# A two-pass product with a 5120 x 5120 matrix: h of a panel interleaved with t of the next, one landing ring, second reads on one queue

## The reference

```python
h = relu(layernorm(x))                                  # 5120 x 64
e = concat(par_u[0]*par_u[1] * (diag_u * h_u @ W_u) + h_u,     # first 2048 rows
           par_i[0]*par_i[1] * (diag_i * h_i @ W_i) + h_i)     # other 3072 rows
g = adj @ (adj.T @ e)                                   # two passes over adj
out = x + layernorm(g) * ln_gamma + ln_beta + h
```

## Time and profile before

| | |
|---|---|
| median of three runs | 540.03 us (538.85 to 540.18) |
| profiled execution | 538.86 us |
| its span | 537.0 us |
| busy: TensorE | 445.0 us, 83% |
| busy: VectorE | 343.5 us, 64% |
| busy: ScalarE | 312.5 us, 58% |
| moved | 139.43 MB, mean 260 GB/s |
| SyncE's queue (q1) | 123.28 MB, 63.1% of 16 engines' span |
| ScalarE's queue (q10) | 15.82 MB, 10.6% |

### The profile page before, as it was taken

One profiled execution on the slowest core, in us unless ns is written; L12 is line 12 of the kernel. 1 busy time (PEld: TensorE's weight loads), 2 busy tenths in 40 slices (PEclk: granted clock), 3 DMA queues, 4 the chain that ended last, 5 costly groups with the idle time before them and its releaser, 6 DMA issues.

```text
span 537.0 us, 5378 instructions
## 1 busy us (share of the span) xinstructions
PE 445.0 (83%) x2108; PEld 179.7 (33%) x2108; DVE 343.5 (64%) x338; ACT 312.5 (58%) x415; POOL 26.9 (5%) x30
## 2 busy tenths in 40 slices
PE   0747554599969989999969799997899898779996
PEld 0313222243423334324423333433343332334433
DVE  2635199473999941499991149999118999701742
ACT  2365830856699924069993207998324699622242
POOL 1011330000000000000000000000000000001132
PEclk9968795899979999999989899998999999799999
DMA  7966109685965979996957699795979968772911
GB/s 222 404 259 264 56 0 379 169 234 165 366 253 214 408 284 206 324 371 253 415 205 281 191 319 372 269 415 206 330 262 315 392 243 338 276 251 63 302 52 59
DMA packets 63112, 139.43 MB, mean 260 GB/s; under 512 B 4208, under 2 KB 37488, under 8 KB 63088
## 3 DMA queue, kind: packets, MB, share of 16 engines
q1 hardware_dynamic: 45360, 123.28, 63.1%
q10 hardware_dynamic: 17728, 15.82, 10.6%
HBM read 137.78 MB, written 1.31 MB: 259 GB/s over the span
## 4 chain that ended last, share of the span: by engine, by line
PE 29%; ACT 22%; DMA 22%; DVE 18%; issue 6%; ACTq 1%; SPq 1%; DVEq 0%
ACT ready L369 20%; DMA nat<-in_adj_dram 17%; PE tT_ps L673 11%; PE h_ps L731 10%; DVE ready L544 8%; DVE ready L533 7%; PE tr_ps L662 5%; DMA ready<-in_adj_dram 3%; DMA diag_sb<-in_L_gnn_diag_i_dram 2%; ACT ready L379 1%; PE tr_ps L710 1%; PE tT_ps L686 1%; ACTq L239 1%; SPq L239 1%; DVE tT_sb L550 1%
## 5 line engine op out<-in xcount | busy, mean ns | idle before, releaser
L369 ACT ACTIVATE ready<-nat 32x1024 f32<-32x1024 f32 x225 | 237.4, 1055 | 65.2 <-PE h_ps L731 47.0
L673 PE MATMUL tT_ps<-nat,e_sb 128*64 128x512 f32 x800 | 199.6, 646 | 31.8 <-DMA nat<-in_adj_dram 28.9
L544 DVE STREAM_TRANSPOSE ready<-ready 128x2048 f32<-128x2048 f32 x80 | 179.5, 2287 | 24.4 <-ACT ready L369 18.2
L731 PE MATMUL h_ps<-ready,t_quads 128*64 128x512 f32 x640 | 178.4, 604 | 7.9 <-DVE ready L544 7.9
L533 DVE COPY ready<-nat 32x1024 f32<-32x1024 f32 x175 | 121.1, 692 | 8.7 <-PE h_ps L731 6.0
L673 PEld LDWEIGHTS tT_ps<-nat,e_sb 128*64 128x64 f32 x800 | 62.1, 147 | 141.4 <-issue 101.8
L731 PEld LDWEIGHTS h_ps<-ready,t_quads 128*64 128x64 f32 x640 | 56.9, 139 | 94.5 <-issue 93.2
L379 ACT ACTIVATE ready<-tr_ps 128x512 f32<-128x512 f32 x80 | 44.0, 595 | 71.9 <-PE tr_ps L662 71.7
L731 PE MATMUL h_ps<-ready,t_blocks 128*64 128x512 f32 x160 | 70.0, 593 | 0.7 <-DVE t_blocks L554 0.7
L662 PE MATMUL tr_ps<-ident,nat 128*128 128x128 f32 x320 | 49.0, 302 | 15.2 <-ACT ready L379 15.2
L662 PEld LDWEIGHTS tr_ps<-ident,nat 128*128 128x128 f32 x320 | 38.6, 154 | 47.4 <-issue 27.9
(11 more groups left out here) (54 smaller groups left out, 118.8 us busy)
## 6 DMA issues: line engine op xcount, KB each, us to landing
nat<-in_adj_dram SPq DMA_DIRECT2D x50, 2048.0 KB, 9.6
ready<-in_adj_dram SPq DMA_DIRECT2D x30, 512.0 KB, 10.3
ready<-in_adj_dram ACTq DMA_DIRECT2D x30, 512.0 KB, 10.5
x_sb<-in_x_dram SPq DMA_DIRECT2D x5, 256.0 KB, 8.7
out_dram<-x_sb SPq DMA_DIRECT2D x10, 128.0 KB, 1.8
ready<-in_L_gnn_W_u_dram SPq DMA_DIRECT2D x2, 16.0 KB, 10.1
ready<-in_L_gnn_W_i_dram SPq DMA_DIRECT2D x2, 16.0 KB, 9.3
gamma_sb<-in_L_gnn_ln_gamma_dram ACTq DMA_DIRECT2D x1, 32.0 KB, 2.6
```

The lines of the kernel that those rows point to most:

```text
L369: last = nc.scalar.activation(dst, src, ACT.Copy)
L544: last = nc.vector.transpose(part, part)
L673: last = nc.tensor.matmul(tT_ps[half * D:(half + 1) * D, :], e_sb[:, g * RB + r, :], nat_slot(p, g)[:, r, half * BANK:(half + 1) * BANK], ...
L731: last = nc.tensor.matmul(h_ps[k][half * D:(half + 1) * D, :], t[:, b, :], tile, start=(p == 0 and b == 0), stop=True, skip_group_check=True)
```

## The change

The same work is cut and ordered in another way.

- `KIND`: groups 0, 5, 8 are read a second time, 1, 2, 3, 4, 6, 9 are moved (six, not five), 7 alone is turned by TensorE. `BANKS` pairs (2,4), (0,1), (3,6), (5,9), (7,8).
- ScalarE takes 8 to 10 of the 16 blocks of a move, by group (`ACT_MOVES`), 53 a panel.
- Buffers: `landing`, a ring of 5 slots for natural and second reads in the one order `LOADS`; `kept`, 7 slots, one for each group that is not read twice. In panel 0 two natural reads (5, 6) land in slots of `kept` (`EARLY`). A second read is turned in its landing slot and holds it until its bank of h is summed.
- All natural reads go out on SyncE's queue, all four transfers of each second read on ScalarE's.
- TensorE's order alternates banks of h of panel p with groups of t of panel p + 1. Both turns of t come before bank 0.
- `t_quads` and `t_blocks` are copied by ScalarE, not VectorE.
- In the head ScalarE's first move goes in pieces of three blocks, the weights and second unit of x are read ahead of the first group, and the moves of groups 6 and 9 of panel 0 come after t. In the tail all turns come ahead of the first `norm_h`.

```diff
-    KIND = ("read", "move", "read", "move", "read", "move", "turn", "move", "turn", "move")
+    KIND = ("read", "move", "move", "move", "move", "read", "move", "turn", "read", "move")
     MOVES = tuple(g for g in range(GROUPS) if KIND[g] == "move")
-    TURNS = tuple(g for g in range(GROUPS) if KIND[g] == "turn")
+    TURN = KIND.index("turn")
     READS = tuple(g for g in range(GROUPS) if KIND[g] == "read")
-    BANKS = ((1, 3), (5, 7), (6, 9), (0, 8), (2, 4))
-    H_ORDER = (1, 3, 5, 7, 9, 6, 8, 0, 2, 4)
-    FIRST_ORDER = tuple(range(GROUPS))
-    NATURAL = 4
-    TURNED = 8
-    ACT_MOVES = 9
+    KEPT = tuple(g for g in range(GROUPS) if KIND[g] != "read")
+    BANKS = ((2, 4), (0, 1), (3, 6), (5, 9), (7, 8))
+    LANDING = 5
+    ACT_MOVES = {1: 8, 2: 10, 3: 9, 4: 8, 6: 8, 9: 10}
     MOVE_BLOCKS = tuple((a, b) for b in range(NQ) for a in range(NQ))
     BATCH = 2
-    BATCHES = tuple((g, b) for g in TURNS for b in range(0, BLOCKS, BATCH))
-    BESIDE_FIRST = {(7, 0): 0, (7, 1): 1, (8, 0): 2, (8, 1): 3, (9, 0): 4, (9, 1): 5}
-    BESIDE = {(6, 0): 0, (6, 1): 1, (7, 0): 2, (7, 1): 3, (8, 0): 4, (8, 1): 5}
-    HELD = (6, 7)
+    EARLY = {5: 6, 6: 9}
+    LOADS = [(0, g, False) for g in range(GROUPS) if g not in EARLY]
+    for p in range(PANELS):
+        LOADS.append((p, READS[0], True))
+        if p < LAST:
+            LOADS += [(p + 1, 0, False), (p + 1, 1, False), (p + 1, 2, False)]
+        LOADS.append((p, READS[1], True))
+        if p < LAST:
+            LOADS.append((p + 1, 3, False))
+        LOADS.append((p, READS[2], True))
+        if p < LAST:
+            LOADS += [(p + 1, g, False) for g in range(4, GROUPS)]
...
-        nat = sb("nat", [P, NATURAL, SLOT])
-        ready = sb("ready", [P, TURNED, SLOT])
+        landing = sb("landing", [P, LANDING, SLOT])
+        kept = sb("kept", [P, len(KEPT), SLOT])
...
+        def landing_slot(p, g, second):
+            return landing[:, LOADS.index((p, g, second)) % LANDING, :]
+        def nat_rows(p, g):
+            slot = kept_slot(EARLY[g]) if p == 0 and g in EARLY else landing_slot(p, g, False)
+            return slot.rearrange("p (r c) -> p r c", r=RB)
+        def turned_rows(p, g):
+            return landing_slot(p, g, True) if KIND[g] == "read" else kept_slot(g)
...
+        def wait_landing_free(eng, p, g, second):
+            n = LOADS.index((p, g, second)) - LANDING
             if n >= 0:
-                p0, g0 = n // GROUPS, order(n // GROUPS)[n % GROUPS]
-                eng.wait_ge(t_summed, t_count(p0, g0))
-                if KIND[g0] == "move":
-                    eng.wait_ge(moved_act, move_count(p0, g0))
-                    eng.wait_ge(moved_dve, move_count(p0, g0))
-                if KIND[g0] == "turn":
-                    eng.wait_ge(tr_filled, tile_count(p0, g0) + BLOCKS)
-        def wait_ready_free(eng, p, g):
-            n = p * GROUPS + H_ORDER.index(g) - TURNED
-            if n >= 0:
-                eng.wait_ge(h_summed, h_count(n // GROUPS, H_ORDER[n % GROUPS]))
-        EGO = ready[:, TURNED - 1, :]
-        w_blk = ready[:, TURNED - 2, 0:2 * P].rearrange("p (s m) -> p s m", s=2)
-        FREE = nat[:, loads_before(LAST, READS[-2]) % NATURAL, :]
-        c_blk = nat[:, loads_before(LAST, READS[-1]) % NATURAL, 0:P]
-        cg_blk = nat[:, loads_before(LAST, READS[-1]) % NATURAL, P:2 * P]
+                p0, g0, second0 = LOADS[n]
+                if second0:
+                    eng.wait_ge(h_summed, h_count(p0, g0))
+                else:
+                    eng.wait_ge(t_summed, t_count(p0, g0))
+                    if KIND[g0] == "move":
+                        eng.wait_ge(moved_act, move_count(p0, g0))
+                        eng.wait_ge(moved_dve, move_count(p0, g0))
+                    if KIND[g0] == "turn":
+                        eng.wait_ge(tr_filled, tile_count(p0) + BLOCKS)
+        def wait_kept_free(eng, p, g):
+            if p:
+                eng.wait_ge(h_summed, h_count(p - 1, g))
+                return
+            if g in (TURN, KEPT[-1]):
+                eng.wait_ge(e_ready, PAIRS)
+            for g0, at in EARLY.items():
+                if at == g:
+                    eng.wait_ge(t_summed, t_count(0, g0))
+                    if KIND[g0] == "move":
+                        eng.wait_ge(moved_act, move_count(0, g0))
+                        eng.wait_ge(moved_dve, move_count(0, g0))
...
-            def second(p, g):
-                sp.wait_ge(t_summed, t_count(p, g))
-                if p == 0 and g == READS[0]:
-                    sp.wait_ge(e_ready, PAIRS)
-                wait_ready_free(sp, p, g)
-                load_second(sp, p, g, range(0, NQ // 2))
             load_x(0)
-            natural(0, 0)
+            load_x(1)
             sp.wait_ge(w_zeroed, 1)
             for s, W in enumerate((W_u, W_i)):
                 for half in range(2):
                     sp.dma_start(w_blk[half * D:(half + 1) * D, s, half * D:(half + 1) * D], W[:, :]).then_inc(w_in, 16)
-            for u in range(1, PAIRS):
+            natural(0, 0)
+            for u in range(2, PAIRS):
                 load_x(u)
-            for g in FIRST_ORDER[1:]:
+            for g in range(1, GROUPS):
                 natural(0, g)
-            for p in range(PANELS):
-                second(p, READS[0])
-                if p < LAST:
-                    natural(p + 1, H_ORDER[0])
-                second(p, READS[1])
-                second(p, READS[2])
-                if p < LAST:
-                    for g in H_ORDER[1:]:
-                        natural(p + 1, g)
+            for p in range(1, PANELS):
+                for g in range(GROUPS):
+                    natural(p, g)
...
             def second(p, g):
-                act.wait_ge(t_summed, t_count(p, g))
-                if p == 0 and g == READS[0]:
-                    act.wait_ge(e_ready, PAIRS)
-                wait_ready_free(act, p, g)
-                load_second(act, p, g, range(NQ // 2, NQ))
+                wait_landing_free(act, p, g, True)
+                load_second(act, p, g, range(NQ))
...
+            def take_quads(p):
+                act.wait_ge(t_turned, 2 * p + 1)
+                if p:
+                    act.wait_ge(h_summed, p * PAIRS)
+                nc.scalar.activation(t_quads[:, :, :], rows64(tT_ps[:, :]), ACT.Copy).then_inc(quads_ready, 1)
+            def take_blocks(p):
+                act.wait_ge(t_turned, 2 * p + 2)
+                if p:
+                    act.wait_ge(h_summed, h_count(p - 1, TURN))
+                nc.scalar.activation(t_blocks[:, :, :], rows64(tT_ps[:, :]), ACT.Copy).then_inc(blocks_ready, 1)
...
+                if u + 1 < PAIRS:
+                    squares(u + 1)
                 egoT_copy(u)
-                if u == 0:
-                    squares(1)
-                if u == 1:
-                    move(0, MOVES[0])
-                if u == 3:
-                    move(0, MOVES[1])
+                if 1 <= u < PAIRS - 1:
+                    move(0, 1, 3 * (u - 1), min(3 * u, ACT_MOVES[1]))
...
+            move(0, 2)
+            move(0, 3)
+            move(0, 4)
+            second(0, READS[0])
             turn_back(0, 0)
             turn_back(0, 1)
+            take_tT(0)
             turn_back(0, 2)
             for p in range(PANELS):
+                take_quads(p)
+                turn_back(p, 3)
+                take_blocks(p)
+                if p == 0:
+                    move(0, 6)
+                move(p, 9)
+                second(p, READS[1])
                 if p < LAST:
+                    move(p + 1, 1)
+                second(p, READS[2])
+                if p < LAST:
+                    move(p + 1, 2)
+                    move(p + 1, 3)
+                    move(p + 1, 4)
                     second(p + 1, READS[0])
+                    turn_back(p + 1, 0)
+                    move(p + 1, 6)
+                    turn_back(p + 1, 1)
                     take_tT(p + 1)
+                    turn_back(p + 1, 2)
...
+            move(0, 1)
+            move(0, 2)
+            turn_moved(0, 1)
+            move(0, 3)
+            turn_moved(0, 2)
+            move(0, 4)
+            turn_moved(0, 3)
+            turn_moved(0, 4)
+            take_tT(0)
             for p in range(PANELS):
                 if p == 0:
+                    move(0, 6)
+                move(p, 9)
+                turn_read(p, READS[0])
+                turn_moved(p, 6)
+                turn_moved(p, 9)
                 if p == LAST:
                     break
+                move(p + 1, 1)
+                move(p + 1, 2)
+                turn_read(p, READS[1])
+                move(p + 1, 3)
+                turn_read(p, READS[2])
+                turn_moved(p + 1, 1)
+                move(p + 1, 4)
+                turn_moved(p + 1, 2)
+                turn_moved(p + 1, 3)
+                move(p + 1, 6)
+                turn_moved(p + 1, 4)
+                take_tT(p + 1)
...
```

(113 more changed lines are left out.)

161 lines of the change are left out of this document (64 added, 97 removed).

## The result

The changed kernel takes 511.6 us (511.09 to 517.03, 4 runs) against 540.11 of before beside it: ratio 0.949, 95% interval 0.943 to 0.956. The forecast was 516 with a range of 478 to 540. The profiled execution took 511.77 us with a span of 510.0, which is what the sum of 514 us of span is held against.

The account below looks back on a forecast made before the run. No single engine bounded the kernel; after the change the late second read of group 8 would. Head 84, first panel 100, three panels of 90 and tail 60 gave 514 us of span, plus 1.9: 516, range 478 to 540.

Parts of the forecast that it names:

- The deciding step: Transfers: second reads on ScalarE's queue alone run at 211 GB/s, 10.1 us each, plus 5.4 per natural read beside them.
- Rival A: Transfers: the one queue costs nothing, second reads take 6.1 us, period 79, total 470 us; chance 0.15.
- The period: A steady panel: group 8 lands at 50.5 us, then 33.8 of VectorE and 3.9 to bank 0; 88.2, taken as 90.
- the third natural read beside it: In a steady panel: natural read 5, released by move 2 at 35 us, delays group 8's landing by 5.4 us.
- SP's ring gives no other stall: In a panel: natural 0 is released by move 6, 8 us before the panel starts and 22 before its t.
- 12 issues, 0.55 each: ScalarE in a panel: 12 transfers issued instead of 6, adding 3.3 us, part of it beside its copies.
- about 70 us: ScalarE's work in a panel after the change, with more copies and issues and fewer tiles to empty.
- The head: Ahead of the first h: e complete at about 41 us, bank 0 starts at 84, not 118.8.
- Rival C: Head keeps its length, e chain paced by TensorE and ScalarE; 551 us at worst, 530 at half; chance 0.06.
- The first panel: Panel 0: moves 6 and 9 come after t, one after the other, so it takes 90 + 10 = 100 us.
- The tail: After the last panel's start: second reads 5 and 8 start at 12.9, 8 lands at 34.2; 60 us instead of 47.5.
- Rival B: Panels: a late group 8 lets natural reads 6 and 7 go beside it; period 99, total 553 us; chance 0.09.

Follow-up runs that it names:

- e1: The changed kernel with each second read issued half by SyncE and half by ScalarE; 481.68 us, ratio 0.891.
- e4: The changed kernel with three of the four transfers of every second read left out, h computed from other data; 465.77 us, ratio 0.859.
- e3: The changed kernel with all second reads issued by SyncE between the natural ones, none by ScalarE; 500.44 us, ratio 0.923.
- e11: The changed kernel itself, run and profiled again on the same chip; 511.39 us.
- e7: The changed kernel with GpSimd's five additions of beta held back until group 4 of t of panel 1 is summed; 511.13 us.
- e5: The kernel before with all four transfers of each second read on ScalarE's queue, none on SyncE's; 615.43 us, ratio 1.141.
- e8: The changed kernel with the last panel's second reads of groups 5 and 8 issued ahead of ScalarE's move of group 9; 519.84 us.
- e9: The changed kernel with second reads halved over both queues and beta's additions behind the head; 474.62 us, ratio 0.879.
- e2: The changed kernel with all four transfers of each second read issued by GpSimd, none by ScalarE; 635.34 us, ratio 1.173.

## Why the prediction was right, and where its sizes were off

**The transfers.** The deciding step held: rates measured apart in the trace of before came back in the changed kernel, and the period is that of a group-8 read landing late. e1 and e4 show it: with a faster path for these reads the steady periods fall to 79 to 85, and with a quarter of them read to 76. Rival A's sum falls, and with it that of the Trainium skill's rule (DMA: Bandwidth & Descriptors, "Issuing engines are not separate DMA queues"). Spreading the 1 KB packets over two queues is worth 30 us here (e1), and 19 of them remain against e3, where ScalarE spends no time on issues.

**The period**, 90 forecast, 86.8 measured. Group 8 landed at 45.2 to 45.9, not 50.5. The term that failed is the third natural read beside it, 5.4 us. In the panel shown natural 5 was issued at 324.6, 44 us into the panel and not 35, because ScalarE's move 2, which releases it, was held by the stand of 11 us. Without it the forecast's own sum gives 12.9 + 20.3 + 2 x 5.4 + 1.1 = 45.1. Behind the landing came 40.3 to 41.7 us and not 37.7. VectorE waited 2.5 to 4.3 for t, since TensorE stood twice in its last groups: 0.7 to 1.9 us for the tiles that ScalarE empties behind its issues for group 0, and 1.2 to 3.3 for natural 9.

```profile
352.50 1.06 PE L691 MATMUL tr_ps<-ident,landing 128*128 128x128 f32 x8 [0.71 <-ACT kept L393]
358.31 3.65 PE L701 MATMUL tT_ps<-landing,e_sb 128*64 128x512 f32 x16 [1.17 <-DMA landing<-in_adj_dram]
```

Natural 9 is released by move 4, which ScalarE ended at 342.7, and landed 15.5 us later at 358.3, beside the second read of group 0. "SP's ring gives no other stall" was thus wrong, and left out these waits. They are what scatters: in e11 TensorE stood 2.4 and 5.7 us for natural 9 in the panels of 90.5 and 89.7, and VectorE 6.5 and 7.3 for t.

```profile
359.04 5.48 PE L701 MATMUL tT_ps<-landing,e_sb 128*64 128x512 f32 x16 [5.72 <-DMA landing<-in_adj_dram]
```

**The signs.** VectorE's longest wait of a panel was to stand at group 8. It did in the first panel (9.5 us) and in the one shown (5.4 against 5.0); in the two others it stood at group 5.

**ScalarE's issues.** "12 issues, 0.55 each" was the step that missed a wait. The long ones come late in a row, as the eighth (14.15 us), or as the fourth for group 0 (6.3 to 7.4) beside two natural reads. What exactly holds the issuer no run shows. The stand both delays ScalarE and spares group 8 a collision, so the error in the period stayed small partly by luck. ScalarE's "about 70 us" was also no sum of its terms: 57.4 + 8.5 - 4.8 + 1.2 + 3.3 is 65.6, and without the issues 62.3, which is what the stretches show (62.3 to 62.5).

**The head**, 84 forecast, 96.9 measured, outside its sign of 80 to 90. e was complete at 48.2 and not 41. Unit 0 ended at 18.6 and not 16.7, and the four units behind it took 7.4, 8.8, 7.8 and 5.6 us, where the forecast counted three of 8 to 9. Some 2 us of the delay are scatter, since e was complete at 46.5 in e11, where TensorE's granted clock was 1.00 from 40 to 48 us and not 0.85. Then come the 4.9 us of copies beside GpSimd, a term that the forecast didn't have and e7 shows, and 0.8 us more between VectorE's last turn and bank 0. Rival C was right in direction for the 7 us, and wrong in size.

**The first panel** (96.4 for 100) was 9.6 us longer than the mean of the others, as forecast; in e11 it was 4.7 longer, so the agreement is in part luck. **The tail**: VectorE waited for 5 and 8 as forecast, 2.0 and 5.1 us; 8 landed 27.6 us in and not 34.2, and 56.3 came out instead of 60. The first issue went out 6.2 us into the tail and not at 11.3. The forecast took over the panel's condition, the slot of group 9; in the last panel no natural reads come between, and the slots are those of groups 6 and 7, free by then. e1's tail of 50.1 fits landings that pace it.

**Rival B** did not come. Natural 6 needs bank 3 of h, which ended at 322.7 in the panel shown, and behind natural 5 it went out only at 325.2, 0.7 us before group 8 had landed.

**What the gain is made of** stays in part open. The head and the panels became shorter about as forecast, and e5 and e1 show what the queue costs, but the interleaved order, the ring, the kinds and the head weren't run one by one.

## What to carry to other kernels

Measure a queue's rate by the packet size that it carries and with what lies beside it: 1 KB packets from one queue moved at 215 GB/s, from two at 348, and beside 4 KB packets at 65. Before moving transfers to an engine that also computes, count what is still on its queue when it issues the next one; it may stand there for 11 us and more, where an issue on a short queue takes half of one. The rest of the change was worth 60 us with both queues and 104 with one, the interleaved order among it. In such an order the input that lands last can set the period, so put the slow read where it is needed late.

## What the runs showed of the hardware

- In the changed kernel an issue of a 512 KB read in 1 KB pieces took 0.32 to 0.65 us in most cases, 14.15 us with six others of its queue not yet landed, and 6.3 to 7.4 us as the fourth in a row beside two natural reads. Eight in a row took 27.85 us in e5 beside natural reads and 10.26 in e8 without them.
- A natural read issued at 294.23, right behind ScalarE's four, moved no packet before 300.9: from 294 to 300 only ScalarE's queue was active.
- Five additions of GpSimd (128 x 512) took 8.31 us beside VectorE's copies. Five of the copies took 1.65 to 1.68 us then, and 0.69 otherwise. In e7 the additions ran beside VectorE's transposes and took 6.17 us, and the transposes took their usual 4.50 and 4.46; in e9 they ran beside copies again and took 7.99. The Trainium skill (SBUF — State Buffer, "SBUF: two separate sides") has the two engines share one pair of ports under an exclusive lock; the trace agrees for the copies, five of which were held beside five additions.
- GpSimd's 512 KB transfers landed 6.9 us after their issue in the median, but GpSimd idled 4 to 10 us ahead of each issue in the stretch shown, and e2 was the slowest kernel. VectorE ran only transposes for part of it.
